# Linear-attention scores in 64-row tiles, with eight query blocks and PSUM laid out head, chunk, query

## The reference

```python
xc = silu(causal_depthwise_conv(layernorm(x)))
q, kg, v, g = xc @ wq, xc @ wkg, xc @ wv, xc @ wg + bg     # q, kg: 64 wide; v, g: 128 wide
gk = log_sigmoid(kg) / 16;  k = 1 - exp(gk)                # 8 heads of 8 (q, k) and of 16 (v)
S[t] = S[t-1] * exp(gk[t]) + k[t] (outer) v[t]             # for each sequence and head
o[t] = (q[t] / sqrt(8)) @ S[t]
o = o + sigmoid(sum(q * aug * k) * v)
x = x + (silu(g) * groupnorm(o)) @ wout
```

## Time and profile before

| what | value |
|---|---|
| median of 3 runs | 335.25 us (335.13 to 338.85) |
| span of the profiled execution, first to last instruction | 332.2 us |
| what lies around the span, by the median | about 3 us |
| mean granted TensorE clock | 0.993 |
| busy: PE, ACT, DVE, PEld, POOL | 284.2, 245.3, 241.6, 204.6, 164.5 us |
| records of PE matmuls | 3672 |

### The profile page before, as it was taken

One profiled execution on the slowest core, in us unless ns is written; L12 is line 12 of the kernel. 1 busy time (PEld: TensorE's weight loads), 2 busy tenths in 40 slices (PEclk: granted clock), 3 DMA queues, 4 the chain that ended last, 5 costly groups with the idle time before them and its releaser, 6 DMA issues.

```text
span 332.2 us, 9709 instructions
## 1 busy us (share of the span) xinstructions
PE 284.2 (86%) x3672; PEld 204.6 (62%) x3672; DVE 241.6 (73%) x604; ACT 245.3 (74%) x438; POOL 164.5 (50%) x226
## 2 busy tenths in 40 slices
PE   1686679989899989988999999999998999888861
PEld 1575537665568666855786568656865676456461
DVE  1577987689687877887779957895679558555555
ACT  6399869886988699759976997789787866773521
POOL 5146366845564446573857283737471525012640
PEclk9999999999999999999999999999999999999997
DMA  2830200020003000210011000400020001001010
GB/s 74 236 94 18 67 0 2 14 70 2 1 14 82 7 2 12 72 32 2 10 39 37 2 8 21 106 0 6 14 65 2 6 8 49 2 0 34 2 32 17
DMA packets 15726, 10.46 MB, mean 31 GB/s; under 512 B 2816, under 2 KB 13952, under 8 KB 15680
## 3 DMA queue, kind: packets, MB, share of 16 engines
q1 hardware_dynamic: 15680, 9.84, 11.2%
HBM read 4.79 MB, written 2.10 MB: 21 GB/s over the span
## 4 chain that ended last, share of the span: by engine, by line
PE 47%; ACT 15%; issue 15%; DVE 14%; POOL 5%; SPq 3%; DMA 1%; POOLq 0%; DVEq 0%; ACTq 0%
PE S L823 7%; PE PT L860 7%; PE PB L881 7%; PE AT L746 6%; PE PA L765 5%; ACT prT L1265 3%; ACT pr L1258 3%; DVE at L1572 3%; PE S L838 3%; PE PT L646 2%; ACT L1182 2%; PE PA L781 2%; DVE nmax L1626 2%; SPq L296 2%; PE PA L646 2%
## 5 line engine op out<-in xcount | busy, mean ns | idle before, releaser
L1626 DVE TENSOR_REDUCE nmax<-S 128x16 bf16<-128x1024 f32 x31 | 37.8, 1219 | 27.7 <-PE S L823 27.4
L1265 ACT COPY prT<-PT 128x512 f32<-128x512 f32 x62 | 36.1, 582 | 15.8 <-PE PT L860 14.8
L860 PEld LDWEIGHTS PT<-ident,pr 128*128 128x128 f32 x248 | 26.4, 140 | 28.8 <-issue 18.6
L860 PE MATMUL PT<-ident,pr 128*128 128x128 f32 x248 | 39.9, 283 | 3.9 <-ACT prT L1265 1.3
L1146 ACT ACTIVATE k_bd<-S,k_rows 128x512 f32<-128x512 f32 (+1 forms) x72 | 41.8, 644 | 0.2
L881 PEld LDWEIGHTS PB<-v_x,prT 128*64 128x64 f32 x992 | 32.8, 137 | 8.1 <-issue 6.8
L881 PE MATMUL PB<-v_x,prT 128*64 128x18 f32 x992 | 37.3, 213 | 0.5 <-ACT prT L1265 0.2
L486 POOL TENSOR_TENSOR kc<-ke,e_r 128x512 f32<-128x512 f32 x32 | 35.9, 1140 | 3.5 <-issue 3.5
L823 PE MATMUL S<-k_bd,qT 64*64 64x512 f32 x248 | 33.8, 615 | 4.3 <-ACT pr L1258 2.5
L1258 ACT ACTIVATE pr<-S,rs 128x1024 f32<-128x1024 f32 x31 | 34.5, 1114 | 3.4 <-PE S L838 3.1
L746 PE MATMUL AT<-q_bd,kc 128*64 128x128 f32 x512 | 31.4, 275 | 2.0 <-issue 1.4
(11 more groups left out here) (171 smaller groups left out, 669.5 us busy)
## 6 DMA issues: line engine op xcount, KB each, us to landing
cT<-in_ctxT SPq DMA_DIRECT2D x7, 256.0 KB, 3.5
v_bd<-vt SPq DMA_DIRECT2D x28, 64.0 KB, 2.1
out<-yout SPq DMA_DIRECT2D x7, 256.0 KB, 2.4
q_bd<-qs SPq DMA_DIRECT2D x96, 8.0 KB
cT<-in_ctxT SPq DMA_DIRECT2D x2, 128.0 KB, 3.0
x_all<-in_x SPq DMA_DIRECT2D x1, 256.0 KB, 3.0
v_bd<-vt SPq DMA_DIRECT2D x8, 32.0 KB, 1.9
out<-yout SPq DMA_DIRECT2D x2, 128.0 KB, 1.9
```

The source lines that it names most:

```text
L860: last = nc.tensor.transpose(dst[:, P * p:P * p + P], pr_v[:, i % 2, P * (hp * n + p):P * (hp * n + p) + P], ident[:, :])
L1265: nc.scalar.copy(prT[:, 512 * n:512 * n + 512], pt_buf(g, n)[:, :]).then_inc(s_prT, 1)
L1626: nc.vector.tensor_reduce(nmax[:, XH * (i % 2):XH * (i % 2) + XH], cut(s_buf(g, i), XH, L), AX.X, ALU.max, negate=True).then_inc(s_max, 1)
```

## The change

The score matmuls are cut by row halves: for each chunk, tile and half one matmul over 64 partitions, with 8 blocks (the heads) of 8 queries as its 64 moving columns. `q_bd` has H = 8 blocks; block h holds head h of both halves, each in its own partitions, and zeros elsewhere. The results of the two halves go to columns 0 to 511 and 512 to 1023 of `AT`, in the order head, chunk, query, so that the tile lies as `at` does and the mask reads and writes contiguously. `first_blocks` multiplies by the 8 columns of `k_rows` (made by DVE as the sum of the two halves of `block_of`, 1 where the partition belongs to head h of either half) in place of the 16 of `block_of`, and waits for `k_mask`. The 16 DMAs of a later group write to block `n % H`.

```diff
--- before.py
+++ after.py
@@ -135,14 +135,13 @@
         qs, ke, qkp = sb("qs", KH), sb("ke", KH), sb("qkp", KH)
         kc = sb("kc", TPG * NCH * L)
         kc_m = cut(kc, TPG, NCH, L)
-        q_bd = sb("q_bd", NB * KH)
-        q_bdv = cut(q_bd, NB, KH)
+        q_bd = sb("q_bd", H * KH)
+        q_bdv = cut(q_bd, H, KH)
         vt = sb("vt", GT)
         v_bd = sb("v_bd", 2 * 2 * 2 * E)
         v_bdv = v_bd[:, :].rearrange("p (j x w f) -> p j x w f", j=2, x=2, w=2)
         at = sb("at", 2 * NB * L)
         at_m = cut(at, 2, NB, L)
-        at_c = at[:, :].rearrange("p (j n c s) -> p j c n s", j=2, n=NB, c=NCH)
         gh, tg, sg = sb("gh", GT), sb("tg", GT), sb("sg", GT)
         z, tz, o_s, dev, sq1, on = (sb(n, GT) for n in ("z", "tz", "o_s", "dev", "sq1", "on"))
         osum, oss, lnv, ors = (sb(n, TPG * H) for n in ("osum", "oss", "lnv", "ors"))
@@ -180,6 +179,7 @@
         PA0, PA1, AT = ps("PA0", 512), ps("PA1", 512), ps("AT", 1024)
         S, PT, PB = ps("S", 1024), ps("PT", 512), ps("PB", 512)
         AT0, AT1 = AT[:, 0:512], AT[:, 512:1024]
+        AT_m = cut(AT, NB, L)
 
 
         w_in, w_keys, w_later, x_in, x_rest, c_even, c_odd = (
@@ -275,7 +275,7 @@
                 sp.wait_ge(s_qs, g + 1)
                 sp.wait_ge(s_AT, pairs(g))
                 for n in range(NB):
-                    sp.dma_start(q_bdv[8 * n:8 * n + 8, n, 0:kcols(g)], qs[8 * n:8 * n + 8, 0:kcols(g)]).then_inc(s_qbd, 16)
+                    sp.dma_start(q_bdv[8 * n:8 * n + 8, n % H, 0:kcols(g)], qs[8 * n:8 * n + 8, 0:kcols(g)]).then_inc(s_qbd, 16)
 
             def values_to_blocks(g):
                 sp.wait_ge(s_vt, g + 1)
@@ -743,10 +743,12 @@
                 for c in range(NCH):
                     for w in range(2):
                         i = 2 * j + w
-                        last = nc.tensor.matmul(AT[L * w:L * w + L, c * NB * CH:(c + 1) * NB * CH],
-                                                kc_m[:, i, c, :],
-                                                q_bdv[:, :, L * i + CH * c:L * i + CH * c + CH],
-                                                start=True, stop=True)
+                        for half in range(2):
+                            rows = slice(L * half, L * half + L)
+                            last = nc.tensor.matmul(AT_m[L * w:L * w + L, H * half:H * half + H, CH * c:CH * c + CH],
+                                                    kc_m[rows, i, c, :],
+                                                    q_bdv[rows, :, L * i + CH * c:L * i + CH * c + CH],
+                                                    start=True, stop=True)
                 last.then_inc(s_AT, 1)
 
             def attend(g, j, part):
@@ -761,9 +763,8 @@
                 o_v = PA1[:, 0:cols(g)].rearrange("p (j w f) -> p j w f", w=2, f=E)
                 for h in heads:
                     for half in range(2):
-                        n = H * half + h
                         last = nc.tensor.matmul(o_v[L * half:L * half + L, j, :, DVH * h:DVH * h + DVH],
-                                                at_m[:, j, n, :], v_bdv[:, j, half, :, DVH * h:DVH * h + DVH],
+                                                at_m[:, j, H * half + h, :], v_bdv[:, j, half, :, DVH * h:DVH * h + DVH],
                                                 start=True, stop=True)
                 if part == 1:
                     last.then_inc(s_AV, 1)
@@ -1553,9 +1554,9 @@
                 dve.wait_ge(s_qs, g + 1)
                 if part == 0:
                     dve.wait_ge(s_AT, pairs(g))
-                    dve.wait_ge(consts2, 10)
-                for n in range(NB // 2 * part, NB // 2 * part + NB // 2):
-                    last = nc.vector.tensor_scalar(q_bdv[:, n, 0:kcols(g)], qs[:, 0:kcols(g)], block_of[:, n:n + 1], None,
+                    dve.wait_ge(k_mask, 1)
+                for h in range(H // 2 * part, H // 2 * part + H // 2):
+                    last = nc.vector.tensor_scalar(q_bdv[:, h, 0:kcols(g)], qs[:, 0:kcols(g)], k_rows[:, h:h + 1], None,
                                                    ALU.mult)
                 if part == 1:
                     last.then_inc(s_qbm, 1)
@@ -1568,8 +1569,8 @@
                 if g == 0 and j == 0:
                     dve.wait_ge(at_clear, 1)
                     dve.wait_ge(derived, 1)
-                mask = cut(causal, NCH, CH).unsqueeze(2).to_broadcast([P, NCH, NB, CH])
-                nc.vector.copy_predicated(at_c[:, j, :, :, :], mask, cut(AT, NCH, NB, CH)).then_inc(s_at, 1)
+                mask = causal[:, :].unsqueeze(1).to_broadcast([P, NB, L])
+                nc.vector.copy_predicated(at_m[:, j, :, :], mask, AT_m).then_inc(s_at, 1)
 
             def a_aug(g):
                 dve.wait_ge(s_AUG, g + 1)
```

## The result

The changed kernel takes 332.42 us (median of 20 runs, lowest 329.72); the kernel before, on the same chip, 335.28 us. The ratio is 0.9886, with an interval of 0.9856 to 0.9916: 1.1% faster, a gain of 2.9 us where 7.8 were forecast. It is outside the likeliest case's own range (326 to 329.5) and inside the full one (325.3 to 333.0). The profiled execution took 332.23 us, span 330.5 us. Ratios are taken without the executions in a slower state (among them single ones of 394 to 652 us, with every matmul slow), while medians are of all executions.

What follows compares the result with a forecast made beforehand. The prediction took the kernel as bound by the order of TensorE's work, with hand-overs to other engines. Gains of 3.0 + 3.7 + 0.8 + 0.4 = 7.9 us cut the span from 332.2 to 324.3, hence 327.5 us; range 325.3 to 333.0.

Steps and rivals of the forecast that it cites:

- the likeliest case: Whole kernel: short calls and the gain reaching the end give 327.5 us, own range 326 to 329.5; chance 0.65.
- The mechanism: Score matmuls: four 64x64 tiles run beside each other, a call takes 0.97 us in place of 1.78, saving 0.81.
- the change of form: TensorE's short wait when the tile form changes, around scores(a, 1): it only moves in front of the call, zero.
- The first rival: Score matmuls: second row half does not run beside the first; call 1.94 us, 334.5 us in all; chance 0.18.
- its milder form: Score matmuls: 25 ns floor between starts for all tiles, call 1.6 us, about 331.5 us; a third of 0.18.
- the slower one: Score matmuls: short records sharing a half run four in a row, 3.5 us a call, about 358 us; chance 0.04.
- All three are just ahead, so a step gives 0.73 us of 0.81: Steady steps: waits behind scores(a, 1) end just ahead of the shorter call; groups 2 to 6 give 3.7 us.
- the 0.8 of group 7: Group 7: 0.1 us at its first mask and 0.7 from the second score call, 0.8 us together.
- The three covers: Steady step: mask waiting for DVE's y, x_scores for ACT's k_bd, xn transposes for POOL; 0.1 us or less away.
- The second rival: Steps: call gets faster but a moved cover holds the gain, 0.3 us a step, 330 us; chance 0.13.
- The granted clock is 1.00 over the first 30 us [...] I count nothing for it: Opening: new idle of 1.5 to 1.8 us before attend is not much longer than the existing 1.35; no clock loss.
- The forecast of 3.0: Opening, groups 0 and 1: fewer DVE blocks and shorter calls give 3.0 us by ACT's exponential of group 1.

Runs made afterwards that it cites:

- e4: Changed kernel with the loop over the two row halves outermost in the score matmuls, same 64 records a call: 335.76 us, ratio 1.0008.
- e10: Changed kernel with GpSimd's scale_a(n + 5) behind scale_b2(a) and ACT's last piece of k_bd ahead of its aug work: 330.70 us, ratio 0.9861.
- e13: Changed kernel with extra TensorE matmuls at nine places of the opening, no new order, run again for its profile: 330.80 us, ratio 0.9866.
- e2: Changed kernel with GpSimd's order alone, scale_a(n + 5) moved behind scale_b2(a) in each step: 332.72 us, ratio 0.9892.
- e11: Changed kernel with ACT's order alone, the last piece of k_bd ahead of its aug work: 332.83 us, ratio 0.9908.
- e12: Changed kernel with extra TensorE matmuls in the opening and both GpSimd's and ACT's new orders, repeated: 329.33 us, ratio 0.9819.

## Why the prediction was wrong

*What held.* The mechanism: four tiles beside each other, 1.09 us a call where 0.97 was forecast and the change of form put at nothing beside it, so 0.69 us saved for each call on the chain in place of 0.81. The mask took what it did, and the DMAs and the attend index show no cost. The first rival (1.94 us a call) is what e4 shows with another loop order (its milder form, given as 331.5 us, comes out at 330.9 by the same sum: 335.25 - 2.4 - 11 x 0.18); the slower one is out.

*The step that failed: "All three are just ahead, so a step gives 0.73 us of 0.81. Groups 2 to 6: 5 x 0.73 = 3.7 us".* Over the five steps behind `x_scores(1, 0)` (groups 3 to 7, of which the last is the 0.8 of group 7) that makes 4 x 0.73 + 0.8 = 3.7 us; the changed kernel gained 1.58. The three covers were read off one step, 175 to 182 us, and the one that decides there was not among them: GpSimd's reciprocals in front of the exponential, 0.77 us ahead in the kernel before. In four of the other five places k_bd was only 0.38 to 0.42 us ahead of `x_scores`, not the 0.71 of the one read. e10 shows it: with both moved, three of the five steps give 0.63 to 0.71 us and a fourth 0.59, near the forecast, and the sum is 2.75. The two waits are thus 1.2 of the 2.1 us missing in these steps; most of the other 0.9 is missing in the first step, where it stays open. The second rival, "the gain stays in the step" through k_bd or GpSimd's chain, was the right one for the steps: its 0.3 us a step is what was measured (1.58 / 5). It gave 330 us at a chance of 0.13, and the opening took the rest.

*"The granted clock is 1.00 over the first 30 us [...] I count nothing for it".* The new idle time of 1.63 us before `attend` was followed by a stretch at 1.2 GHz in which L708 took 1.92 us. By `x_scores(1, 0)`, with the call of group 2 in it, 3.7 us were forecast; 1.7 came, and 3.0 where no such stretch fell behind 25 us (e13). The Trainium skill (TensorE: Matmul & The Clock Gate, "HAM oscillation — how this bites in real kernels") warns of idle gaps in TensorE's work. Here the gap alone does not decide: the same 1.63 us stand before `attend` in e10, where the clock falls behind them (0.84 from 25 to 36 us), and in e2 and e11, where it does not (1.00). So what the clock takes varies from execution to execution, in both kernels: the mean clocks of their runs are 0.973 and 0.977.

*The rest of the opening.* `scores(0, 0)` starts at 26.69, not behind kc, which ends at 25.92, but behind DVE's eight blocks, which end at 26.58: the four last ones, begun while kc is still being made, take 1.35 us, 0.34 each in place of 0.27. And the mask (28.13) no longer follows the call (27.85) but DVE's own statistics and a memset, which end at 28.12. That makes 1.8 us at `attend` in place of 2.3. Further on, even at full clock the gain stood at 2.35 us by `ogT` (67.29 us before, 64.94 in e12), after 3.38 us at `o_s` (58.48, 55.10). The forecast of 3.0 missed that DVE's `sg` would meet GpSimd's `kc`. The changed kernel's timeline:

```profile
64.15 2.56 POOL L486 TENSOR_TENSOR kc<-ke,e_r 128x512 f32<-128x512 f32 x2
...
64.31 1.46 DVE L1522 SCALAR_TENSOR_TENSOR sg<-tg,gh 128x512 f32<-128x512 f32 x1
```

It took 0.68 us in the kernel before, where `sg` started 0.02 us behind `kc` and not 0.16. No run moved it away from `kc` on purpose, so its price of 0.8 us is read, not tested.

*The sum of the profiled execution.* Forecast 7.9 us. Measured 1.7 at `x_scores(1, 0)` (of which 0.7 is already the call of group 2), 1.6 from there to `x_scores(6, 0)`, -0.4 in the step of group 8 (31.34 to 31.77 us), 0 behind it: 2.8 at the last `yout`, and 1.1 of them went to a later landing of the last store. So groups 2 to 7 fell 2.2 us short of their 4.5, the opening 2.0 short of its 3.0, and group 8 0.8 short of its 0.4. That group 8 lost 0.4 us was not repeated in e10 or e13 (31.27 and 31.30), and in e12 it gained 0.5 (30.81).

*What stays open.* The step from `x_scores(1, 0)` to `x_scores(2, 0)` gives 0.15 to 0.24 us in every short-call kernel of the table with GpSimd's order or neither, and 0.65 with ACT's order alone; why GpSimd's order takes that back was not tried. Nor is it known what makes the clock fall at one place and not at another, or where it fell in executions without a profile.

## What to carry to other kernels

Before a saved duration is multiplied by a number of steps, look at the slack of every wait behind it in each of these steps, down to the next place where all engines meet; one step's slack is no one's price, and 0.3 us of slack missing in a step takes 0.3 us of the gain. When 64x64 matmuls are to run beside each other, the order of the loops decides: with the four tiles in turn a call took 1.09 us, with one row half's matmuls all ahead of the other's 1.91 (other orders were not tried). Where an edit makes TensorE finish early in a stretch that is already sparse, leave room in the range for the granted clock, compare medians over many runs, and don't trust one profile of either kernel for the clock.

## What the runs showed that was not expected

Records of 64x64 tiles start far closer than one engine-wide floor would allow: 64 records in 1.09 us are 0.017 us each, with their weight loads. The Trainium skill (TensorE: Matmul & The Clock Gate, "Wait — 56ns, not 53.3ns?") says starts never come closer than about 25 ns; the measurement decides, and in e4, where neighbours share a row half, 0.030 us comes out.

Two engines at work at once can double an instruction's time: GpSimd's reciprocals (L443) take 1.37 us where they start under DVE's `xcT` (L1516, 179.52 to 180.20 us), but 1.01 us in the kernel before, where `xcT` starts 0.48 us behind them; DVE's `sg` takes 0.68 and 1.46 us beside `kc`. Which of the two starts first, and by how much, differs in each pair of places; no run moved one alone. Such meetings appear and vanish when an edit moves the engines by 0.1 to 0.7 us.
